# A graph kernel's node loop: two one-hots built by eight 16-bit row comparisons each, in place of one comparison over all eight blocks

## The reference

```
h = relu(layernorm(x))
agg = segment_sum(h[src] * edge_weight, dst)              # the messages, summed at their target node
x = x + agg @ W_neigh + b_neigh + h @ W_self.T
h = relu(layernorm(x))                                    # used for its shape alone
seg_sum, seg_max, seg_mean of edge_attr (32 wide) by src  # 0 where a node has no edge
h = relu(concat(seg_sum, seg_max, seg_mean, u[0]) @ W1 + b1)
x = x + h @ W2 + b2
```

## Time and profile before

| | |
|---|---|
| median of the runs | 2242.63 us |
| profiled execution: time, span | 2241.82 us, 2240.10 us |
| busy share of the span: PE, DVE, ACT, POOL | 56%, 72%, 22%, 49% |
| granted TensorE clock, mean over the span | 0.641 |
| granted TensorE clock, 1095 to 2230 us | 0.75 |
| node loop, 1095 to 2230 us: DVE busy, PE busy | 949.19 us, 849.07 us |

### The profile page before, as it was taken

How to read it: one execution, slowest core, us unless ns; L and a number is a source line. 1 busy time by engine, 2 the same in 40 slices (tenths; PEclk the granted TensorE clock), 3 DMA queues, 4 the chain that set the end, 5 groups by cost and what they waited for, 6 DMA issues and landing times. The chain is left out here.

```text
span 2240.1 us, 41882 instructions
## 1 busy us (share of the span) xinstructions
PE 1258.9 (56%) x14884; PEld 1073.5 (48%) x14885; DVE 1617.5 (72%) x3568; ACT 494.4 (22%) x888; POOL 1101.9 (49%) x1404
## 2 busy tenths in 40 slices
PE   4566565400001444433277777777777777777775
PEld 3444443300000333322266666667676666666665
DVE  5766767810068888766488888888888888888886
ACT  1221211100000211111132333333332333333332
POOL 7777777777773777777222222222222222232220
PEclk7565555555555555555577777777777777777776
DMA  9700000100063222222545555555555555555551
GB/s 263 95 13 13 12 13 13 55 28 13 13 154 82 76 76 79 73 61 67 104 109 122 125 119 120 125 123 121 124 119 123 123 118 124 118 123 126 119 123 32
DMA packets 405256, 203.62 MB, mean 91 GB/s; under 512 B 370375, under 2 KB 377799, under 8 KB 404407
## 3 DMA queue, kind: packets, MB, share of 16 engines
q1 hardware_dynamic: 254792, 93.02, 19.4%
q0 software_dynamic: 46976, 72.79, 14.3%
q10 hardware_dynamic: 103312, 35.54, 6.3%
HBM read 138.46 MB, written 62.73 MB: 90 GB/s over the span
## 5 line engine op out<-in xcount | busy, mean ns | idle before, releaser
L592 POOL DMA_INDIRECT xg_all<-in_x_dram,idx_src x391 | 385.9, 987 | 149.4 <-issue 118.3
L598 POOL DMA_INDIRECT by_win<-rows,idx_win x391 | 391.2, 1000 | 127.3 <-issue 127.3
L969 POOL DMA_DIRECT2D rows<-by_win x98 | 52.2, 532 | 782.4 <-DVE arena L1000 753.7
L1110 PE MATMUL ps<-arena,w1r 32*128 32x192 f32 x2352 | 214.2, 526 | 267.8 <-DVE arena L1000 264.6
L1110 PEld LDWEIGHTS ps<-arena,w1r 32*128 32x128 f32 x2352 | 164.6, 302 | 280.1 <-DVE arena L1000 276.6
L974 POOL DMA_DIRECT2D rows<-flag_d x392 | 214.4, 554 | 13.7 <-issue 13.6
L1122 PE MATMUL ps<-w_sb,arena 128*96 128x64 f32 x1568 | 185.8, 285 | 0.0
L1122 PEld LDWEIGHTS ps<-w_sb,arena 128*96 128x96 f32 x1568 | 184.4, 203 | 0.0
L1197 ACT ACTIVATE arena<-ps,hbias 128x768 f32<-128x768 f32 x98 | 88.3, 901 | 413.0 <-PE ps L1110 413.0
L417 ACT ACTIVATE sq<-xc 128x512 f32<-128x512 f32 x147 | 91.6, 623 | 364.7 <-DVE xc L399 364.7
L427 PE MATMUL ps<-ident,h 128*128 128x128 f32 x196 | 54.6, 434 | 174.4 <-DVE h L412 174.4
(11 more groups left out here) (191 smaller groups left out, 2840.9 us busy)
## 6 DMA issues: line engine op xcount, KB each, us to landing
rows<-message SPq DMA_DIRECT2D x784, 36.4 KB, 2.0
rows<-flag_d POOLq DMA_DIRECT2D x392, 72.0 KB, 2.6
rows<-in_x_dram SPq DMA_DIRECT2D x97, 256.0 KB, 3.1
out_dram<-rows ACTq DMA_DIRECT2D x97, 256.0 KB, 2.8
message<-m_row SPq DMA_DIRECT2D x48, 388.0 KB, 2.3
zeros<-slot_d POOLq DMA_DIRECT2D x98, 144.0 KB, 2.9
by_win<-zeros ACTq DMA_DIRECT2D x12, 808.5 KB, 10.6
arena<-by_win SPq DMA_DIRECT2D x7, 1386.0 KB, 9.4
```

The lines of the kernel that those rows point to most:

```text
L592: nc.gpsimd.indirect_dma_start(out=xg[g % RX][:, t % GT, :], out_offset=None, in_=x, in_offset=bass.IndirectOffsetOnAxis(ap=idx_src[:, t:t ...
L598: nc.gpsimd.indirect_dma_start(out=by_win, out_offset=bass.IndirectOffsetOnAxis(ap=idx_win[0:parts, t:t + 1], axis=0), in_=rows[0:parts, t ...
L1110: last = nc.tensor.matmul(ps[z_bank[q]][:, 0:2 * SL], w1r[DE * q:DE * q + DE, j, :], part[DE * q:DE * q + DE, :], start=(j == 0), stop=(j ...
```

## The change

Each of the two comparisons over 8 x 128 elements becomes eight comparisons over 128 elements. Each of the eight reads the row 0 to 127 as bfloat16 (`iota_b`, 128 whole numbers that the type holds exactly, made once ahead of the loop by a cast into storage of the gathered rows that is free by then), and compares it with one float32 number per lane, a scalar operand read from SBUF. The outputs, their type and their place are as before, and so are the waits; the signal to PE is given by the last of the eight.

```diff
@@ storage @@
+        iota_b = xg_all[:, 0:P // 2].bitcast(BF16)
@@ select(g) @@
-                    nc.vector.tensor_tensor(sel[g % 2][:, :, :], iota_n[0:SL, :].unsqueeze(1).to_broadcast([SL, GT, P]),
-                                            end_n[:, g * GT:g * GT + GT].unsqueeze(2).to_broadcast([SL, GT, P]),
-                                            ALU.is_equal).then_inc(w["sel"], 1)
+                    for k in range(GT):
+                        last = nc.vector.tensor_scalar(sel[g % 2][:, k, :], iota_b[0:SL, :],
+                                                       end_n[:, g * GT + k:g * GT + k + 1], None, ALU.is_equal)
+                    last.then_inc(w["sel"], 1)
@@ picks(g) @@
-                    nc.vector.tensor_tensor(pick[c][0:CH, :, :], iota_n[0:CH, :].unsqueeze(1).to_broadcast([CH, GT, P]),
-                                            near[c][:, :].unsqueeze(2).to_broadcast([CH, GT, P]),
-                                            ALU.is_equal).then_inc(w["pick"], 1)
+                    for k in range(GT):
+                        last = nc.vector.tensor_scalar(pick[c][0:CH, k, :], iota_b[0:CH, :], near[c][:, k:k + 1], None,
+                                                       ALU.is_equal)
+                    last.then_inc(w["pick"], 1)
@@ ahead of permute(0) @@
+                own(nc.vector.tensor_copy(iota_b, iota_n[:, :]))
```

## The result

The changed kernel takes 2278.18 us (median of 4 runs, 2275.71 to 2288.12) against 2242.74 us of the kernel before (2241.53 to 2244.96): ratio 1.0165, 95% interval 1.0133 to 1.0198. It is 35 us slower; the forecast said 10 us slower, and the range ended at 2274. The profiled execution is the longest of the four, 2288.12 us with a span of 2286.4 us. The runs of before lie within 3.4 us, those of the changed kernel spread over 12.

The account below looks back on a forecast made before the run. PE was taken to bound every group, with DVE 0.2 us short of it in about 65 and 2.2 us in about 33. 65 x 0.155 = 10.1 us on 2241.8 gives 2251.9, median 2252.5, range 2239 to 2274.

Parts of the forecast that it names:

- What bounds the kernel: Node loop, L1000 to L1039: PE sets the time; DVE alone needs 6.20 us and waits 0.19 or 0.22, sometimes 2.19.
- short groups: About 65 groups of the node loop, L1000 to L1039 in 6.39 or 6.42 us, forecast to become 6.56.
- long ones: About 33 groups, one in three, where DVE waits 2.19 us for PE, whose granted clock is 0.50; period 12.76 us.
- The price of one comparison: New DVE comparison: duration 245 ns, spacing 166 ns; eight cost 1.32 us in place of 1.14, 0.36 us more per group.
- the two rows without the operand: DVE rows L1061 and L724, with no scalar operand from SBUF: fixed parts of 159 and 160 ns beside their columns.
- rival (d): Node loop, L398 on DVE: GpSimd holds it up once per group by 0.23 us, +15 us, 2267 us; chance 0.07.
- In 33 groups the 2.19 us wait hides the 0.36: Where DVE waits 2.19 us for PE, its stretch growing by 0.36 us per group adds nothing to the time.
- the sum: Whole kernel: 65 groups at 0.155 us more give 10.1 us; 2241.8 + 10.1 = 2251.9 us for the profiled execution.
- Rival (b): PE clock and ring: slow groups one in 2.5, 2265 us (0.18); fewer, 2237 (0.06); rhythm held, 2243 (0.05).
- The median: Median of the runs 0.8 us above the profiled execution: 2252.7, predicted 2252 to 2253, say 2252.5 us.
- (a): Scalar operand's read hidden in a chain: spacing 105 ns, eight take 0.84 us, PE still sets 2242 us; chance 0.18.
- (c): New comparisons run two per clock: spacing 198 ns, 0.88 us more per group, +45 us, 2288 us; chance 0.06.

Follow-up runs that it names:

- e1: Kernel before with only the comparison of select(g) split into eight, the one in picks(g) kept; 2626.00 against 2628.06 us, ratio 0.999.
- e2: Kernel before with only the comparison of picks(g) split into eight, the one in select(g) kept; 2630.95 against 2628.06 us, ratio 1.001.
- e3: Changed kernel with the number k in the instruction instead of the SBUF scalar in all sixteen comparisons, output not right; 2628.39 against 2628.06 us, ratio 0.9992.
- e9: Kernel before plus one unused DVE instruction of 32 columns (0.11 us) per group ahead of L1039; 2646.48 against 2649.99 us, loop 1110.9 us.
- e12: Changed kernel run once more, on another chip, beside the kernel before; 2670.31 against 2649.99 us, ratio 1.0087, loop 1145.8 us.
- e10: Kernel before plus one unused DVE instruction of 175 columns (0.26 us) per group ahead of L1039; 2662.06 against 2649.99 us, loop 1124.0 us.
- e6: Kernel before plus 24 constant matmuls per group where PE is idle, behind neighbours(g); 2562.49 against 2646.07 us, ratio 0.9683, loop 1020.7 us.
- e7: Changed kernel plus 24 constant matmuls per group where PE is idle, behind neighbours(g); 2596.33 us against 2646.07 of the kernel before, ratio 0.9803, loop 1054.3 us.

## Why the prediction was wrong, step by step

- What bounds the kernel: right. PE sets the stretch by 0.19 us in short groups and by 2.2 in long ones; e1, e2, e3 and e9 bear it out.
- The price of one comparison: right, 166 ns forecast and 163 measured from start to start. The operand's read is not hidden in a chain (61 ns by e3, 50 worked out). How the rest divides into columns and fixed part is worked out and not measured: with 33 ns of columns the duration of 184 ns in e3 leaves 151, near the 159 and 160 of the two rows without the operand. The rule of the Trainium skill that gives about 75 ns per instruction ("Vector Engine (DVE) Microarchitecture Reference", Measured stream behaviour on trn2) nearly holds for the immediates (102 - 33 = 69 ns) and not with a scalar operand (163 - 33 = 130 ns).
- The short groups: right in size, 6.54 for 6.56 us. In the first profile 24 of the 45 have 6.66, by rival (d), GpSimd's hold-up, at 0.13 us a time and not 0.23. The row of 180 ns at most was taken for a sign that plain DMAs rarely hold L398 up; it showed only that L398 stood at 0.07 us, ahead of the place where it is held.
- "In 33 groups the 2.19 us wait hides the 0.36": right for a long group (its stretch stays 8.47 us, the wait falls to 1.73 where L398 is held too), and this is where the sum failed. It took the number of long groups, 33, as given. It is 53 in the profiled execution, which is 38 of the 47.5 us, and 49 in e12.
- Rival (b) named the mechanism and stopped at one long group in 2.5, +12 us. It became one in 1.9 to 2. Its size was guessed from a small shift, because I thought of a rhythm that changes its count by a little, and it got a chance of 0.18 and no part in the sum. The fixed rhythm of three gives way as soon as the slack is used up. Before, a long wait of PE closes the sum of three periods at 34.14 us again and again; the two short waits of 0.19 and 0.22 us may be what lets it close, since a group that comes a little late has its wait shortened. With DVE the bound in the short groups that play is gone. That the two waits hold the rhythm is my reading of e1, e2, e9 against e10, and not shown; the counts show the edge at the slack, the traces that long groups are those at the low clock, and e6 and e7 that they go when the clock is kept up. Why the clock falls in just these groups stays open.
- The median: 35 us over before. e12's loop, without hold-ups, is 34 to 38 us over 1108 to 1112, so on the first chip the median may be the lost rhythm and the short groups alone. Against it stands that e12's own median is only 20 us over.
- Rivals (a) and (c) are out: 163 ns is neither 105 nor 198.

## What to carry to other kernels

Where two engines race in a ring and the later one waits 0.2 us, an edit that adds less than this wait is free, and one that adds more can cost several times the part beyond the wait (here 35 us for 10), if the other engine's clock falls when the rhythm changes; so count the slack in the fast groups and test an edit in halves before adding the shares. See first whether the engine that is waited for runs at its high clock: 24 matmuls of constants in its idle time gave 3.2% here, where cheaper DVE instructions (e3) gave nothing. And an estimate that takes a count from the present state, here 33 long groups, needs a reason why the edit leaves the count alone. Eight instructions with a scalar operand replace one of eight times the length only if the added fixed cost is less than what the faster mode saves: here 8 x 0.130 - 0.08 = 0.96 us against some 0.80 us of columns.

## What was not expected of the hardware

- A `tensor_scalar` with its scalar in SBUF costs DVE 163 ns for 128 columns of bfloat16, with an immediate 102 ns.
- In the first profile a DVE stretch that grows by 0.35 us changes the granted TensorE clock of the loop from 0.75 to 0.70, and PE's busy time over the span from 1258.9 to 1307.2 us with the same instructions.
- The cost of DVE work in this loop, one execution each: 0.11 us per group nothing that can be told from e3, 0.26 us 16 us in all, 0.36 us 28, 0.74 us 57; with the clock held at 1.00, 0.35 us costs 33.6.
- POOL's plain DMA instruction of 545 ns holds up a small SBUF-to-SBUF `tensor_scalar` that starts 246 ns or more behind its start, until it ends, and none that starts up to 243 ns behind it: 52 of 98 groups in one execution and none in another.
